# A thought stage with its normalisation behind the first product, and a grouped mixture whose rows are placed choice by choice

## The chip, the cores and the metric

The kernel runs on one core of one Trainium2 chip. The metric is device time in microseconds; the kernel before took 2209.59 us (median of 3 runs, 2209.09 to 2212.38).

## The reference, cut to what matters

Four layers, each with cross attention and a feed-forward part, act on x of 4 batches x 256 tokens x 256. Two of the eight parts are changed.

Layer 1's feed-forward, from the last token of each batch (the "thought"):

```
x_norm = layer_norm(x, in_gamma, in_beta)
thought = x_norm[:, -1, :] @ agg_w + agg_b              # 4 x 256
for _ in range(4):
    t = layer_norm(thought, pn_gamma, pn_beta)
    t = gelu(t @ d1_w + d1_b)                            # 4 x 1024
    thought = thought + (t @ d2_w + d2_b)
gate = sigmoid(x @ gate_w + gate_b)                      # 1024 x 256
out = x + gate * (thought @ bc_w + bc_b)[:, None, :]
x = x + layer_norm(out, out_gamma, out_beta)
```

Here x on the right is the normalised input. Layer 2's feed-forward is a mixture: 64 experts of width 176, of which each token chooses the 6 likeliest, and a shared part of width 352 that all tokens pass:

```
y = silu(x @ w1[e]) @ w2[e]          # for the 6 chosen e, mixed by their shares
shared = (silu(g) * u) @ shared_down # g, u = x @ shared_gate_up
```

All is float32.

## The kernel before, in words

The stages run one after another, each in a block of its own with one instruction list for each engine. A block's end holds all engines; nothing crosses it but DMAs issued ahead. Order within a stage is written out by hand: each engine's list is fixed, and semaphores (`wait_ge`) order the engines against each other. Tokens lie in 8 tiles (TT) of 128 rows; the width of 256 is 2 chunks (DC).

**Thought stage** (`thought_stage`, L1697). SP issues all loads in order, and last the four weights of the next attention (`Products.sync`, 5 MB). VectorE takes the moments of all 8 tiles (`Norm.vector`), then normalises the last tokens twice as 4 rows (`first_rows`, L1935), then the 8 tiles; TensorE transposes these (L199) and ScalarE copies them (L210). Each of the 4 steps is a chain: VectorE's statistics of the 4 thought rows, GpSimd's power for the inverse root (L1804), VectorE's rows (L1933), two transposes (`turn`, L1820), ScalarE's gamma and beta (L1901), the product with d1_w with its 4 spans in 4 column groups of TensorE (L1854), the bias on VectorE (L1965), Gelu (L1905), two transposes (L1860), a copy, the product with d2_w in 4 partial sums (L1865), a copy (L1909), and one product that adds the 4 parts (L1871). Behind that, TensorE does the step's two tiles of the gate product (L1833), and VectorE adds the gate's bias (L1949) and out_beta (L1951) in the next step. At the end come bc_w, a product that spreads each batch's row over 128 partitions (L1878), two copies (L1975), GpSimd's 8 products with the gate (L1808), VectorE's final normalisation in two halves (to L1998), and beside it, on TensorE and ScalarE, `Products` for the next attention's 16 heads (L406, L407, L411), in two banks by turns.

**Grouped stage** (`grouped_mixture`, L2198). Routing gives each (token, choice) a slot, with the experts in ascending order in blocks of 128 slots, 111 blocks at most. A token's 6 slots are sorted descending, so choice 0 is the highest. GpSimd writes the normalised rows to their slots with 48 indirect DMAs, tile by tile and in it choice by choice (L2490). Beside them VectorE makes 48 pairs of one-hots (L2580, L2581) that TensorE multiplies (L2396) to know each slot's target row. Then TensorE does the shared experts' outputs of pairs 0 and 1, the inputs of pairs 2 and 3 (L2336; 3 units a pair) and their outputs (L2346). SP loads each block's weights into 6 slots (L2304, L2307), each wait being on the block 6 before. ScalarE waits for all 48 placements (L2446), loads the rows of blocks 0 to 5 (L2444), and in the loop those of block b + 6. For each block TensorE transposes the rows (`turn`, L2354; two blocks ahead), multiplies (`up`, L2366; one ahead) and again (`down`, L2374, L2375); VectorE copies x_t (L2631), ScalarE applies silu (L2455) and copies y (L2464), GpSimd scatters y (L2496), behind its last placement.

Of the kernel before, what the change touches and what calls it, by code (L numbers as in the profile page):

```python
# [12 lines left out]
ACT = mybir.ActivationFunctionType  # L13
# [6 lines left out]
P = 128  # L20
# [93 lines left out]
class Norm:  # L114
# [29 lines left out]
    def vector(self, dve, between=None, after=None):  # L144
        m = self.m
        for n in range(self.SETS):
            of = self.set_of(n)
            for t in of:
                last = dve.bn_stats(self.stats[:, t, :], m.x[:, t, :])
            last.then_inc(self.stats_done, 1)  # L150
            dve.wait_ge(self.stats_done, n + 1)
            for t in of:
                last = dve.bn_aggr(self.moments[:, t, :], self.stats[:, t, :])
            last.then_inc(self.moments_done, 1)
            dve.wait_ge(self.moments_done, n + 1)
            at = slice(of[0], of[-1] + 1)
            dve.tensor_scalar(self.spread[:, at], self.moments[:, at, 1], self.EPS, None, ALU.add).then_inc(self.spread_done, 1)

        if between:
            between()  # L160
# [21 lines left out]
    def gpsimd(self, pool):  # L182
        for n in range(self.SETS):
            at = slice(self.set_of(n)[0], self.set_of(n)[-1] + 1)
            pool.wait_ge(self.spread_done, n + 1)
            pool.tensor_tensor(self.rstd[:, at], self.spread[:, at], self.m.minus_half[:, at], ALU.pow).then_inc(self.rstd_done, 1)
# [197 lines left out]
class Products:  # L384
# [4 lines left out]
    def __init__(self, st, m, dram, banks):  # L389
        self.m, self.banks = m, banks  # L390
# [7 lines left out]

    def tensor(self, pe, h):
# [3 lines left out]
        wait_for(pe, self.product_kept, h + 1 - len(self.banks))  # L403
        bank = self.banks[h % len(self.banks)]
# [4 lines left out]
    def scalar(self, act, h):  # L409
        act.wait_ge(self.product_made, h + 1)  # L410
        act.copy(self.m.products[:, h, :], self.banks[h % len(self.banks)][:]).then_inc(self.product_kept, 1)  # L411
# [1285 lines left out]
def thought_stage(nc, m, dram, of_heads):  # L1697


    eps = 1e-6  # L1700
# [5 lines left out]
    IN_GAMMA, IN_BETA, AGG_B, D2_B, BC_B = range(5)  # L1706
    small_names = ("in_gamma", "in_beta", "agg_b", "d2_b", "bc_b")
    GATE_B, OUT_GAMMA, OUT_BETA = range(3)
    wide_names = ("gate_b", "out_gamma", "out_beta")
    with Stage(nc, m, "l1f") as st:  # L1710
# [5 lines left out]
        to_group = st.sbuf("to_group", [chunks, span // P, groups, ROWS])  # L1716
# [1386 lines left out]
```

## Time and profile before

| What | us |
| --- | --- |
| Median of 3 runs | 2209.59 |
| The profiled execution | 2207.66 |
| Its span | 2205.9 |
| Thought stage, 822.9 to 906.8 | 83.9 |
| Hidden sums of its steps start | 846.4, 857.8, 868.5, 879.1 |
| Grouped stage's first placement, first block's transposes | 1290.1, 1357.3 |

A row of a timeline is the start in us, how long, engine, line, operation, output and inputs by the program's names, shapes and how many records; in brackets the idle time before it and what released it. A float32 product leaves two records. PEclk is TensorE's granted clock as a share of 2.4 GHz. A stretch's row gives busy time for each engine. The profile was taken on one execution.

### The profile page before, as it was taken

The page shows a single profiled execution, that of the slowest core. Times are in us where ns is not written, and L with a number is a line of the kernel's source. Part 1 is how long each engine was busy: PE and PEld are TensorE (multiplying, and loading weights), DVE is VectorE, ACT ScalarE, POOL GpSimd, SP SyncE. Part 2 cuts the span into 40 slices and gives each one's busy share as a digit, 9 for nine tenths or more (in the row PEclk, how much of TensorE's full clock was granted, in tenths as well). Part 3 has the DMA queues.
Part 4 walks back from the last instruction along what each step waited for, and adds up shares of the span by engine and source line. Part 5 has one row for each costly group of instructions (what it writes and reads, how often), then busy time and mean ns, then how long its engine had stood idle before and what let it go on. Part 6 is the DMA issues. An engine that isn't in the chain of part 4 may idle for free. (4 is left out here: it accounts for less than half of the span.)

```text
span 2205.9 us, 43116 instructions
## 1 busy us (share of the span) xinstructions
PE 1994.0 (90%) x13031; PEld 1709.7 (78%) x13031; DVE 1500.8 (68%) x4243; ACT 1153.0 (52%) x2626; POOL 678.8 (31%) x1298
## 2 busy tenths in 40 slices
PE   5798796989999986799999885999879999988998
PEld 3544485779999983699999774999769999976887
DVE  6788576858878883788888772322268888875565
ACT  3656443756766752566666411444246666653333
POOL 3422102013333310333334155544323333312221
PEclk9899898999999996899999897999989999988999
DMA  2157302012212104520000024999810000014441
GB/s 67 33 109 196 129 1 72 2 56 71 78 52 78 56 17 155 183 88 0 0 0 0 29 95 159 315 318 315 282 41 23 14 21 14 15 32 122 117 116 39
DMA packets 145257, 193.66 MB, mean 88 GB/s; under 512 B 45084, under 2 KB 113284, under 8 KB 142216
## 3 DMA queue, kind: packets, MB, share of 16 engines
q1 hardware_dynamic: 119912, 152.40, 23.1%
q10 hardware_dynamic: 17584, 18.82, 2.6%
q0 software_dynamic: 7632, 20.85, 2.5%
q8 instruction: 66, 1.08, 0.2%
q14 instruction: 63, 0.52, 0.1%
HBM read 169.86 MB, written 56.62 MB: 103 GB/s over the span
## 5 line engine op out<-in xcount | busy, mean ns | idle before, releaser
L2631 DVE COPY l2f_x_t<-bank 128x256 f32<-128x256 f32 x111 | 47.1, 424 | 178.5 <-PE bank L2354 178.5
L2496 POOL DMA_INDIRECT l2f_y_rows<-l2f_y,l2f_target x111 | 111.6, 1005 | 115.9 <-ACT l2f_y L2464 113.7
L705 ACT ACTIVATE l1a_prob<-l1a_masked,l1a_shift,l1a_q_scale 128x512 f32<-128x512 f32 x128 | 104.5, 816 | 76.2 <-DVE l1a_shift L763 74.1
L705 ACT ACTIVATE l2a_prob<-l2a_masked,l2a_shift 128x512 f32<-128x512 f32 x128 | 92.8, 725 | 78.5 <-DVE l2a_shift L767 75.8
L705 ACT ACTIVATE l3a_prob<-l3a_masked,l3a_shift 128x512 f32<-128x512 f32 x128 | 92.7, 725 | 78.4 <-DVE l3a_shift L767 75.7
L2366 PE MATMUL bank<-l2f_x_t,l2f_w 128*128 128x128 f32 x888 | 118.4, 277 | 0.2 <-DVE l2f_x_t L2631 0.2
L1315 ACT ACTIVATE l0a_prob_t<-bank 128x512 f32<-128x512 f32 x128 | 76.2, 599 | 64.5 <-PE bank L1253 63.7
L2366 PEld LDWEIGHTS bank<-l2f_x_t,l2f_w 128*128 128x128 f32 x888 | 109.0, 193 | 0.6 <-issue 0.5
L1332 DVE TENSOR_REDUCE l0a_coarse<-bank 128x32 f32<-128x512 f32 x128 | 87.5, 688 | 26.1 <-PE bank L1243 24.4
L757 DVE CUSTOM_DVE_ANT_0 l3a_masked<-bank,l3a_side 128x512 f32<-128x512 f32 x128 | 88.4, 691 | 14.1 <-issue 12.8
L757 DVE CUSTOM_DVE_ANT_0 l2a_masked<-bank,l2a_side 128x512 f32<-128x512 f32 x128 | 88.4, 691 | 11.7 <-issue 10.4
L757 DVE CUSTOM_DVE_ANT_0 l1a_masked<-bank,l1a_side 128x512 f32<-128x512 f32 x128 | 88.4, 690 | 9.9 <-issue 8.6
L2699 POOL TENSOR_TENSOR l3f_low<-l3f_raw,l3f_high 128x768 fp32r<-128x768 f32 x24 | 44.3, 1848 | 160.5 <-ACT l3f_high L2694 160.5
L2455 ACT ACTIVATE l2f_h<-bank 128x128 f32<-128x128 f32 x111 | 30.8, 277 | 114.5 <-PE bank L2366 114.5
L2918 DVE TENSOR_TENSOR l3f_upped<-l3f_gate,bank 128x512 f32<-128x512 f32 x48 | 33.0, 687 | 78.0 <-PE bank L2819 78.0
L840 POOL TENSOR_TENSOR l3a_pool_woken<-ones 128x1 f32<-128x1 f32 x90 | 17.4, 193 | 210.8 <-ACT l3a_q_t L689 154.1
L779 DVE TENSOR_TENSOR l1a_prob_low<-bank,l1a_prob_high 128x512 fp32r<-128x512 f32 x128 | 81.1, 675 | 0.1
L779 DVE TENSOR_TENSOR l2a_prob_low<-bank,l2a_prob_high 128x512 fp32r<-128x512 f32 x128 | 81.1, 675 | 0.0
L779 DVE TENSOR_TENSOR l3a_prob_low<-bank,l3a_prob_high 128x512 fp32r<-128x512 f32 x128 | 81.1, 675 | 0.0
L2817 PE MATMUL bank<-l3g_x_high,l3f_high 128*128 128x512 f32 x192 | 75.8, 395 | 3.7 <-PEq L2033 3.7
L840 POOL TENSOR_TENSOR l1a_pool_woken<-ones 128x1 f32<-128x1 f32 x90 | 17.3, 192 | 195.9 <-ACT l1a_q_t L689 147.9
L840 POOL TENSOR_TENSOR l2a_pool_woken<-ones 128x1 f32<-128x1 f32 x90 | 18.3, 203 | 189.9 <-ACT l2a_q_t L689 165.1
(605 smaller groups left out, 7455.1 us busy)
## 6 DMA issues: line engine op xcount, KB each, us to landing
l2f_w<-w_rows SPq DMA_DIRECT2D x111, 304.0 KB
l1a_side<-rms SPq DMA_DIRECT2D x16, 1024.0 KB, 4.8
l2f_x_rows_of<-x_slots ACTq DMA_DIRECT2D x111, 128.0 KB, 3.9
w_rows<-in_l2f_w SPq DMA_DIRECT2D x4, 2048.0 KB
l2f_hots<-l2f_y_rows SPq DMA_DIRECT2D x8, 768.0 KB, 9.9
l3f_raw<-in_l3f_w SPq DMA_DIRECT2D x24, 256.0 KB, 3.8
l3f_mix<-shares SPq DMA_DIRECT2D x16, 384.0 KB, 3.8
l2f_w_rest<-in_l2f_w SPq DMA_DIRECT2D x111, 48.0 KB
```

What stands on the lines that cost most here:

```text
L705: act.activation(prob[:, unit, :], masked[:, unit, :], ACT.Exp, bias=shift[:, unit:unit + 1], scale=q_scale[:, slot, t:t + 1] if qk_norm e ...
L757: dve.tensor_tensor_reduce(masked[:, unit, :], score_bank[q][:], side[:, slot if qk_norm else 0, b * KEYS:(b + 1) * KEYS], 1.0, LOWEST, AL ...
L779: dve.tensor_tensor(prob_low[part], turn_bank[q][:].rearrange("p (n t) -> p n t", n=KT), prob_high[part].bitcast(F32), ALU.subtract).then_ ...
L840: pool.tensor_tensor(pool_woken[:], m.ones[:, 0:1], m.ones[:, 0:1], ALU.mult)
L1315: act.activation(prob_t[:, (2 * g + j) % slots, 2 * half:2 * half + 2, :], turned_bank[u % 2][:].rearrange("p (n t) -> p n t", n=2), ACT.E ...
L1332: dve.tensor_reduce(coarse[:, g % 2, j, q, :], score_bank[n % 3][:].rearrange("p (s k) -> p s k", k=LAST_KEYS), AX_X, ALU.max).then_inc(co ...
L2366: last = pe.matmul(pair_bank[b % 2][:, n * P:(n + 1) * P], w[:, slot, first:first + P], x_t[:, b % 2, c * P:(c + 1) * P], start=(c == 0), ...
L2496: pool.indirect_dma_start(y_rows, bass.IndirectOffsetOnAxis(target[:, b:b + 1], 0), y[:, b % of.Y_SLOTS, :], None).then_inc(y_stored[b % o ...
L2631: dve.tensor_copy(x_t[:, b % 2, :], turn_bank[b % 2][:, 0:D]).then_inc(x_kept, 1)
L2699: pool.tensor_tensor(self.low[:, slot, at], self.raw[:, slot, at], self.high[:, slot, at].bitcast(F32), ALU.subtract).then_inc(self.low_do ...
L2817: pe.matmul(bank[:], left_high, right_high, start=(c == 0), stop=False)
L2918: dve.tensor_tensor(upped[:, n, :], gate[:, n, :], up_bank[n][:], ALU.mult).then_inc(up_done, 1)
```

## The change

Two stages change, and each with several parts.

Thought stage:

- The thought is kept in two forms in two banks: as columns (`columns`, 128 x 2 x 32) and as rows (`thought`, each batch's row in all 32-row groups). Both are sums that TensorE accumulates: bias or residual come in as products with the identity (`ahead_t`, `ahead`), the partial sums with `sum_of` and `sum_all`.
- The normalisation moves behind the product with d1_w: the columns times gamma go in at once, and mean and inverse root are applied to the product, (hidden - mean x sums) x rstd + offsets, in two VectorE instructions. Sums (gamma @ d1_w) and offsets (beta @ d1_w + d1_b) are made once, in step 0.
- The first rows are normalised once instead of twice (the two layer norms folded), ahead of the second set of moments.
- The step's gate tiles go ahead of the transposes of `active`, and heads 0 and 1 of `Products` into steps 2 and 3.
- The end: four products with bc_w on spread columns (`batch_t`), one bank for each batch; VectorE multiplies gate tiles 0 and 1, GpSimd the other 6.
- Loads wait on seven semaphores instead of three; small ones are issued from ScalarE's queue.

Grouped stage:

- Placements go choice by choice, 5 to 0, with a semaphore each. SP loads rows of blocks 0 to 4 (`AHEAD`), block b as soon as choice 5 - b has landed, then weights of blocks 6 to 10, then, when choice 0 has landed, rows of blocks 5 to 10. TensorE does blocks 0 to 4 one after another; the old loop starts at block 5.
- The shared outputs of pairs 0 and 1 come into the one-hot loop at its products 1 and 3, the shared inputs of pairs 2 and 3 at 8, 13, ... 33; VectorE's share of that work comes 6 products later.

```diff
 def thought_stage, tensor:
-                    turn(1 + n)
-                    for c in range(DC):
-                        ... hidden_bank <- rows_t x d1_w
+                    pe.wait_ge(rows_set, n + 2)
+                    past_rows(hidden_bank, lambda c: rows_t[:, c, :]).then_inc(hidden_ready, 1)
+                    if n == 0:
+                        pe.wait_ge(set_up, 5)
+                        past_rows(parts_bank, lambda c: pn_rows[:, PN_GAMMA, c, :]).then_inc(sums_ready, 1)
+                        pe.wait_ge(bias_kept, 1)
+                        past_rows(active_bank, lambda c: pn_rows[:, PN_BETA, c, :], ends=False)
+                        for i in range(inner):
+                            last = pe.matmul(active_bank[:, i * P:(i + 1) * P], to_group[...], d1_rows[:], start=False, ...)
+                        last.then_inc(offsets_ready, 1)
+                        norm.ready(pe)
+                        pe.wait_ge(gate_loaded, 32)
+                    gate_products(step_tiles(n))
+                    for h in range(sum(BEHIND[:n]), sum(BEHIND[:n + 1])):     # BEHIND = (0, 0, 1, 1)
+                        products.tensor(pe, h)
                     pe.wait_ge(active_done, n + 1)
                     ... transposes of active
+                    pe.wait_ge(columns_kept, n + 1)
+                    pe.matmul(columns, m.ident[:], ahead_t[...], start=True, stop=False)
+                    if n + 1 < STEPS1:
+                        pe.wait_ge(rows_kept, n + 1)
+                        pe.matmul(thought, m.ident[:], ahead[:], start=True, stop=False)
                     pe.wait_ge(active_kept, n + 1)
                     ... product with d2_w
                     pe.wait_ge(parts_kept, n + 1)
-                    pe.matmul(row_bank[0:B, 0:D], sum_of[:], parts[:], start=True, stop=True).then_inc(product_ready, 1)
-                    gate_products(step_tiles(n))
+                    for to in range(DC):
+                        last = pe.matmul(columns[:, to * ROWS:(to + 1) * ROWS], parts[:, to * P:(to + 1) * P], sum_of[:], ...)
+                    last.then_inc(thought_ready, 1)
+                    if n + 1 < STEPS1:
+                        pe.matmul(thought, sum_all[...], parts[:], start=False, stop=True).then_inc(rows_ready, 1)
 ...
+                for b in range(B):
+                    if b >= 2:
+                        pe.matmul(said_of(b), ones_row[:], bc_b[:], start=True, stop=False)
+                    pe.wait_ge(batch_set, b + 1)
+                    for c in range(DC):
+                        last = pe.matmul(said_of(b), batch_t[:, b, c, :], weights["bc_w"][:, c, :], start=False, ...)
+                    last.then_inc(said_ready, 1)
+                for h in range(sum(BEHIND), HEADS):
+                    products.tensor(pe, h)
 vector:
+                def turn_thought(n):
+                    dve.wait_ge(thought_ready, n + 1)
+                    dve.tensor_tensor(rows_t[:], columns..., pn_rows[:, PN_GAMMA, :, :], ALU.mult).then_inc(rows_set, 1)
+                def measure_thought(n):
+                    dve.wait_ge(rows_ready, n + 1)
+                    dve.bn_stats(stats[:], thought).then_inc(stats_read, 1)
+                    dve.wait_ge(stats_read, n + 1)
+                    link(dve.bn_aggr(moments[:], stats[:]))
+                    dve.tensor_scalar(spread[:], moments[:, 1:2], eps, None, ALU.add).then_inc(spread_done, 1)
+                norm.take_moments(dve, 0)
+                ... first rows from last_x: one normalisation, gamma, beta
+                norm.take_moments(dve, 1)
+                dve.wait_ge(set_up, 5)
+                turn_thought(0)
+                measure_thought(0)
+                norm.normalise(dve)
                 for n in range(STEPS1):
+                    if n:
+                        turn_thought(n)
+                        measure_thought(n)
                     dve.wait_ge(hidden_ready, n + 1)
+                    link(dve.scalar_tensor_tensor(centred[:], minus_sums[:], moments[:, 0:1], hidden_bank[...], ALU.mult, ALU.add))
+                    dve.wait_ge(rstd_done, n + 1)
+                    dve.scalar_tensor_tensor(hidden[:], centred[:], rstd[:], offsets[:], ALU.mult, ALU.add).then_inc(hidden_set, 1)
+                    dve.tensor_tensor(ahead_t[...], columns..., d2_columns..., ALU.add).then_inc(columns_kept, 1)
+                    if n + 1 < STEPS1:
+                        dve.tensor_tensor(ahead[:], thought, wide[:, D2_B, :], ALU.add).then_inc(rows_kept, 1)
+                    gate_sums(step_tiles(n))
+                    ... in the last step VectorE copies parts; in steps 1 and 2 it adds out_beta to 4 tiles each
 def grouped_mixture, sync:
-                for b in range(blocks):
+                for b in range(of.W_SLOTS):
+                    load_weights(b)
+                for b in range(of.AHEAD):                    # AHEAD = 5
+                    sp.wait_ge(x_placed[chosen - 1 - b], 16 * TT)
+                    load_rows(sp, b)
+                for b in range(of.W_SLOTS, of.W_SLOTS + of.AHEAD):
+                    load_weights(b)
+                sp.wait_ge(x_placed[0], 16 * TT)
+                for b in range(of.AHEAD, of.AHEAD + of.X_SLOTS):
+                    load_rows(sp, b)
+                for b in range(of.W_SLOTS + of.AHEAD, blocks):
                     load_weights(b)
 tensor, behind one-hot product n:
+                        if n in shared_in_at:                # 8, 13, 18, 23, 28, 33: units 6 to 11
+                            shared_in(shared_in_at[n])
+                        if n in shared_out_at:               # {1: 0, 3: 1}
+                            shared_out(shared_out_at[n])
 ...
-                turn(0)
-                turn(1)
-                up(0)
-                for b in range(blocks):
+                for b in range(of.AHEAD):
+                    turn(b)
+                    up(b)
+                    down(b)
+                turn(of.AHEAD)
+                turn(of.AHEAD + 1)
+                up(of.AHEAD)
+                for b in range(of.AHEAD, blocks):
 scalar:
-                act.wait_ge(x_placed, 16 * TT * chosen)
-                for b in range(of.X_SLOTS):
-                    load_rows(b)
 gpsimd:
-                for t in range(TT):
-                    for k in range(chosen):
+                for k in reversed(range(chosen)):
+                    for t in range(TT):
                         pool.indirect_dma_start(x_slots, ..., m.x_n[:, t, :], None).then_inc(x_placed[k], 16)
 vector, behind one-hots n:
+                    if n - of.SHARED_LAG in shared_out_at:   # SHARED_LAG = 6
+                        add_shared(shared_out_at[n - of.SHARED_LAG])
+                    if n - of.SHARED_LAG in shared_in_at:
+                        shared_multiply(shared_in_at[n - of.SHARED_LAG])
```

## Rows read from the trace of the kernel before

**Rows 1.** Page, part 1: busy us (share of span) xinstructions.
```profile
PE 1994.0 (90%) x13031; PEld 1709.7 (78%) x13031; DVE 1500.8 (68%) x4243; ACT 1153.0 (52%) x2626; POOL 678.8 (31%) x1298
```

**Rows 2.** Busy time by stretch: length, each engine busy (x records), clock, DMA.
```profile
822.90:906.80 83.90, 58.45 (x321) 34.64 (x321) 42.19 (x128) 25.46 (x58) 14.27 (x20) 0.72 0.32 103
...
841.00:852.00 11.00, 6.00 (x39) 2.01 (x39) 1.93 (x7) 3.28 (x7) 0.53 (x1) 0.50 1.07 354
```

**Rows 3.** Timeline, thought stage's opening and step 0: start, us, engine, line.
```profile
826.98 0.17 DVE L157 TENSOR_SCALAR l1f_norm_spread<-l1f_norm_moments 128x4 f32<-128x4 f32 x1
...
834.98 4.28 PE L199 MATMUL bank<-ident,l1t_x_n 128*128 128x128 f32 x14
...
844.34 1.93 PE L1854 MATMUL bank<-l1f_d_w,l1f_rows_t 128*32 128x256 f32 x16 [0.75 <-ACT l1f_rows_t L1901]
...
851.84 3.78 PE L1833 MATMUL bank<-l1f_gate_w,l1t_x_t 128*128 128x256 f32 x8
```

**Rows 4.** Line L1965: count, ns min/median/max, first and last start.
```profile
L1965 DVE TENSOR_TENSOR l1f_hidden<-bank,l1f_d_b x4: 423/424/425, 846.4 to 879.1; 128x256 f32<-128x256 f32 x4
```

**Rows 5.** Timeline, thought stage, last step.
```profile
873.96 3.14 PE L1833 MATMUL bank<-l1f_gate_w,l1t_x_t 128*128 128x256 f32 x8
...
875.39 0.53 POOL L1804 TENSOR_TENSOR l1f_rstd<-l1f_spread,minus_half 4x1 f32<-4x1 f32 x1 [10.48 <-DVE l1f_spread L1931]
...
878.01 1.07 PE L1854 MATMUL bank<-l1f_d_w,l1f_rows_t 128*32 128x256 f32 x16 [0.69 <-ACT l1f_rows_t L1901]
...
879.15 0.42 DVE L1965 TENSOR_TENSOR l1f_hidden<-bank,l1f_d_b 128x256 f32<-128x256 f32 x1 [0.99 <-PE bank L1854]
...
880.98 1.07 PE L1865 MATMUL bank<-l1f_d_w,l1f_active_t 128*32 128x256 f32 x16 [0.46 <-ACT l1f_active_t L1907]
...
883.06 1.99 PE L1833 MATMUL bank<-l1f_gate_w,l1t_x_t 128*128 128x256 f32 x8
```

**Rows 6.** Timeline, thought stage's end.
```profile
889.09 1.29 DVE L1975 COPY l1f_said<-bank 128x512 f32<-128x512 f32 x2 [2.08 <-PE bank L1878]
...
890.46 6.25 POOL L1808 TENSOR_TENSOR l1f_gate<-l1f_gate,l1f_said 128x256 f32<-128x256 f32 x8 [14.53 <-DVE l1f_said L1975]
...
894.46 0.59 ACT L411 COPY products<-bank 128x512 f32<-128x512 f32 x1 [0.29 <-PE bank L407]
...
903.28 3.25 DVE L1998 SCALAR_TENSOR_TENSOR x<-l1f_out,l1f_out_rstd,x 128x256 f32<-128x256 f32 x8
...
905.38 0.59 ACT L411 COPY products<-bank 128x512 f32<-128x512 f32 x1 [0.29 <-PE bank L407]
```

**Rows 7.** Busy time by stretch, grouped stage.
```profile
1332.00:1357.00 25.00, 0.03 (x1) 0.00 (x0) 0.42 (x1) 0.00 (x0) 16.47 (x18) 0.60 0.30 102
1400.00:1575.00 175.00, 175.00 (x1241) 161.53 (x1241) 43.89 (x113) 71.01 (x266) 84.45 (x89) 1.00 0.97 314
```

**Rows 8.** Line L2490, the row placements, and their time to landing.
```profile
L2490 POOL DMA_INDIRECT x_slots<-l2g_x_n,l2f_slot_i x48: 956/960/1465, 1290.1 to 1352.7; - x48
...
DMA to landing us min/median/max: 2.4/2.4/4.6
```

**Rows 9.** Timeline, grouped stage.
```profile
1312.18 0.96 POOL L2490 DMA_INDIRECT x_slots<-l2g_x_n,l2f_slot_i  x1 [0.30 <-issue]
...
1316.33 10.52 PE L2336 MATMUL bank<-l2g_x_t,l2f_shared_w 128*128 128x256 f32 x48
...
1326.69 5.34 PE L2346 MATMUL bank<-l2f_shared_w,l2f_shared_h 128*128 128x256 f32 x24
...
1355.11 2.76 ACTq L2444 DMA_DIRECT2D l2f_x_rows_of<-x_slots  x6
...
1357.33 1.09 PE L2354 MATMUL bank<-ident,l2f_x_rows_of 128*128 128x128 f32 x4 [25.29 <-DMA l2f_x_rows_of<-x_slots]
...
1362.89 0.37 ACT L2464 COPY l2f_y<-bank 128x256 f32<-128x256 f32 x1 [0.44 <-PE bank L2375]
```

**Rows 10.** Line L2396, the one-hot products.
```profile
L2396 PE MATMUL bank<-l2f_hots x96: 275/362/555, 1289.8 to 1311.0; 128*128 128x111 f32 x96
```

More of the change, by code:

```diff
@@ L1705, in thought_stage @@
     span = HIDDEN1 // groups
[L1706 to L1709, printed above, removed]
+    inner = span // P
+    GATE_B, OUT_GAMMA, OUT_BETA, D2_B = range(4)
+    PN_GAMMA, PN_BETA = range(2)
+    BEHIND = (0, 0, 1, 1)
     with Stage(nc, m, "l1f") as st:
@@ L1763, in step_tiles @@
+        columns = columns_bank[:, 0:DC * ROWS]
+        thought = thought_bank[:, 0:D]
         def step_tiles(n):
@@ new lines, in _ @@
+                pe.matmul(columns, bias_columns[:], to_chunk[:].rearrange("c g r -> c (g r)"), start=True, stop=False)
+                pe.matmul(thought, ones_row[:], bias_rows[:], start=True, stop=False)
+                pe.wait_ge(turn_kept, 1)
+                for to in range(DC):
+                    for c in range(DC):
+                        last = pe.matmul(columns[:, to * ROWS:(to + 1) * ROWS], weights["agg_w"][:, c, to * P:(to + 1) * P],
+                                         first_t[:, c, :], start=False, stop=(to == DC - 1 and c == DC - 1))
@@ L1840, in _ @@
+                last.then_inc(thought_ready, 1)
+                for c in range(DC):
+                    for g in range(groups):
+                        last = pe.matmul(thought[g * ROWS:(g + 1) * ROWS, :], first_t[:, c, :], weights["agg_w"][:, c, :],
+                                         start=False, stop=(c == DC - 1), tile_position=(0, g * ROWS))
+                last.then_inc(rows_ready, 1)
+                pe.wait_ge(d1_loaded, 96)
                 pe.transpose(active_bank[0:chunks, 0:P], d1_columns[:], m.ident[:]).then_inc(bias_turned, 1)
@@ L1898, in _ @@
+                act.wait_ge(offsets_ready, 1)
+                act.copy(offsets[:], active_bank[:, 0:span]).then_inc(offsets_kept, 1)
                 for n in range(STEPS1):
[L1899 to L1903 removed]
@@ L1913, in _ @@
                     act.activation(gate[:, t, :], raw[:, t, :], ACT.Sigmoid).then_inc(gate_done, 1)
-                for h in range(HEADS):
+                for b in range(1, B):
+                    act.wait_ge(said_ready, b + 1)
+                    act.copy(said[:, b, :], said_of(b)).then_inc(said_kept, 1)
+                for h in range(sum(BEHIND), HEADS):
                     products.scalar(act, h)
@@ L2144 @@
     EARLY = 2
+    AHEAD = CHOSEN - 1
+    SHARED_LAG = 6
     BY_PRODUCT = 3
@@ L2379, in _ @@
                 pe.wait_ge(shared_loaded, 16)
-                shared_in(0)
+                for n in range(of.SHARED):
+                    shared_in(n)
                 pe.wait_ge(masked, 1)
```

428 lines of the change are left out of this document (225 added, 203 removed).

## The prediction

> **What bounds the kernel now.** I read the page first: TensorE is busy for 90% of the span [rows 1], but that is a mean over the whole program, so the question is how busy it is where the change works. Second, busy time by stretches: in the thought stage (822.9 to 906.8) TensorE shows 58 of 84 us at a mean granted clock of 0.72, and in its first step the clock is 0.50, the 1.2 GHz level [rows 2]. Third, the timelines, for what ends each wait. Everything before and behind either stage waits at a block boundary, so a microsecond cut inside one comes off the total.
>
> Thought stage. The four steps form one chain: hidden sums start at 846.4 and for the last time at 879.1, a pitch of 10.9 us [rows 4], with one small instruction at a time. The stage ends at 906.53, VectorE's last update of x (903.28 + 3.25), just behind ScalarE's last product copy at 905.97 [rows 6].
>
> Grouped stage. The 48 row placements on GpSimd start at 1290.1 and the last at 1352.7 [rows 8]; TensorE ends its shared-expert work at 1332.03 (1326.69 + 5.34) and starts the first expert block at 1357.33, after 25.3 us of waiting for rows [rows 9]; from 1332 to 1357 it has 0.03 us of work [rows 7]. The 111 blocks then run on TensorE at 100%: 1241 records in 175 us, 14 records a block, so 1.974 us a block [rows 7].
>
> **The change, thought stage.**
>
> Opening. The first rows now take one normalisation with the two folded together, and VectorE's second set of moments (ending 827.15 before [rows 3]) comes behind them: I put it at 831.0. GpSimd's inverse root and to_group copy follow it (1.5), so the fifth set_up comes at 832.5, VectorE's rows at 832.8, its statistics until 834.3. The token transposes then start at 834.8, against 834.98 before [rows 3]: they are the bound, because ScalarE copies one tile in 0.6 us. They end near 839.5. On ScalarE's queue nine small DMAs that SP issued before (0.45 each) and the Gelu table now stand ahead of its first copy, which I place at 829.3; nothing waits, with some 0.3 to spare, and what they'd hold beyond that, up to the d1_w landing, is in the lower bound. The first hidden sums now need three products with d1_w in place of one: 1.93 us each at the low clock [rows 3], the third nearer 1.5 as I expect the clock to rise, plus the bias product and a copy: 839.5 + 5.9 + 0.5 = 845.9. Gain 0.5; bounds from -2 (pn columns landing late hold both ScalarE and the transposes) to +2.
>
> One step. Before, from the row sum being ready (873.96, where the gates start) to the hidden sums at 879.15 took 5.2 us: statistics, GpSimd's 0.53 root, rows, two transposes with 4 columns, two affine copies, and the product of 1.07 [rows 5]. After, from the column sum: one multiply (0.25), then the product (1.07) beside statistics and root, then the centring of 0.42: 2.05 us. The second half, 879.15 to 883.06, was 3.9 us [rows 5]. After, TensorE has two gate tiles queued between the first product and the transposes: 1.99 us at the full clock [rows 5] against 1.4 us of centring, hidden and Gelu, so the transposes wait 0.45; the identity products that carry the residual add 0.15 beside ScalarE's copy, the column product takes 0.3. So 4.35, and a step is 2.05 + 4.35 = 6.4 us. In steps 2 and 3 a head's product lies there too, 0.9 us, the pitch of ScalarE's copies (894.46 to 905.38 is 12 heads, 0.91 each [rows 6]): 7.3. Hidden 0 to hidden 3: 6.4 + 6.4 + 7.3 = 20.1, against 32.7: gain 12.6. The gate sums and out_beta additions (0.34 to 0.42 each) lie on VectorE beside this; they cost nothing while a step is over 5.5 us.
>
> End. Last hidden to last sum: 3.9 becomes 5.3 (gates and a head in front of the transposes), loss 1.4. Last sum to end: before 883.06 to 906.53, 23.5 us. After, four batches are spread by VectorE and multiplied by TensorE (0.9 each, 0.45 for the late biases), the last ready 5.05 us after the sum; said copies lie on ScalarE. VectorE's end: first gates at 1.85, GpSimd's remaining six products of 0.78 (6.25 for 8 [rows 6]) until 7.7, then adds, statistics, gain and 3.25 of updates: 16.7. The other end: 14 heads behind 5.05 at 0.91, plus a copy: 18.4. So the products are late next and set the end: gain 5.1.
>
> Sum at the full clock: 0.5 + 12.6 - 1.4 + 5.1 = 16.8 us. The clock is the weak term. It rose in the old stage behind each pair of gate tiles (which took 3.78 us at the low clock, 1.99 at full [rows 3, 5]) and fell again within the step. A step is now 90% TensorE (5.8 of 6.4), but its products with 32-column tiles look like those during which it fell. All of it at 1.2 GHz costs 38 us more (below); I take 9% of that, 3.3 us. Gain 13.5; bounds 8 and 19.
>
> **The change, grouped stage.** Shared experts. Before, 21.2 us of shared work stand behind the one-hots: outputs of pairs 0 and 1 (5.3), inputs of pairs 2 and 3 (10.52), their outputs (5.34, to 1332.03) [rows 9]. Only the last 5.3 stay behind. One-hots come every 0.44 us (48 from 1289.8 to 1311.0 [rows 10]) and cost TensorE about 0.28 at full clock (two records at 175/1241), so the loop holds 7.7 us of the 15.9 moved in; the first output runs at the low clock (2.5 more) and VectorE waits for it. The loop ends at about 1321.5, the shared work at 1327; bounds 1326 and 1334.
>
> Blocks ahead. Choice by choice, each choice is 8 issues. The pitch is 1.26 us (1312.18 to 1352.7, 32 issues), so the 40th starts at 1342.6; it lands 2.4 later [rows 8, 9], SP loads block 4's rows and TensorE has them 2.2 us after the issue, as 1355.11 to 1357.33 [rows 9]: 1347.3. A block alone takes at most 5.5 us (1357.33 to 1362.89 [rows 9]) at the low clock. Blocks 0 to 3 fit between 1327 and 1347, block 4 ends by 1352.8, before the last choice lands (1355.1): all five are free. Gain 5 x 1.974 = 9.9.
>
> What it gives back. SP issues the weights of blocks 6 to 10 only behind block 4's rows, from about 1345.5: 5 x 352 KB at 314 GB/s [rows 7] is 5.6 us of transfer beside the last 8 placements and in front of block 5's rows in SP's queue. Behind that wait stand rows 5 to 10 and all later weights. Placements landed in 2.4 us alone and up to 4.6 beside weight loads [rows 8]: between 0 and 2.2 us late; I take 1.0, nearer the median. A warmer clock at block 5 may return up to 1.5. Gain 8.9; bounds 5.5 and 11.5.
>
> A rule that speaks against this: by the Trainium skill, SBUF — State Buffer, "SBUF: two separate sides", a VectorE instruction in a two-port mode locks GpSimd out and so holds up descriptors of its DMAs. The trace agrees: the 16 issues beside the one-hots took up to 1.465 us against 0.956 alone, a pitch of 1.47 against 1.26 (3.1 us lost) [rows 8, 9]. If each placement paid for the longer loop too, the last would start 0.8 us later; as the one-hots stay 96 instructions, I leave the sum as it is.
>
> **Sum.** 13.5 + 8.9 = 22.4 us. The profiled execution took 2207.66 us (span 2205.9): 2185.3. The median is 1.9 above it, so 2187.
>
> **Rivals.**
> 1. The clock stays low in half of the thought stage. For: 0.50 in step 0, 0.72 overall [rows 2]. Against: the gaps that went with it (row normalisation, GpSimd's root) leave TensorE's path. It costs 38/2 less the 3.3 already taken: 15.7 us, total 2203, 0.3% faster.
> 2. Slower: TensorE at 1.2 GHz all through the stage, with gates queued in front of each transpose. Place: product 1.93, gates 3.78 [rows 3], transposes 0.7, identities 1.15, product 1.93, sums 0.6, copies 0.85: 11.5 a step, 13.3 with a head; last sum at 893.3, said 9.2, 14 heads at 1.75, end 927.5: 21 us later than 906.5, less 8.9: 2222. It decides once over two thirds of TensorE's work from 839 on runs low (it may lose 38; both gains at full clock are 25.7). Against: a denser queue than any old step. By the Trainium skill, TensorE: Matmul & The Clock Gate, "What's actually happening", the low clock is the default and recent activity lifts it; that rule gives the full clock here, 2184, and the trace's rise behind dense gate tiles agrees.
> 3. The head start is given back: the last choice and block 5's rows land late by the 2.2 and VectorE's stalls in the loop push the shared work to 1334, so that block 4 ends behind them. Grouped gain 3 to 4, total 2192.
> 4. The change doesn't do what it says: placements by choice don't free early blocks. The waits show they do (block b waits for choice 5 - b alone), so this would be 2196, with little weight.
>
> **How the numbers follow.** Forecast 70% (own range 2178 to 2192); rival 3 and 4 12%; rival 1 10%; rival 2 and milder forms of it 8%. A difference under 0.2% (4.4 us) can't be told from none. Slower: 5%; within 0.2%: 5% (between rivals 1 and 2); faster: 90%. The range 2177 to 2199 leaves out rivals 1 and 2.
>
> **What would show it.** Hidden sums' starts (centring) at pitches of 6.4, 6.4 and 7.3, first at 846; 10 would refute the step. Granted clock near 0.9 from 850 on. The stage's last instruction a product copy, not VectorE's update, near 893. First block at 1327 (shifted by the thought gain), a gap before block 4, and block 5 at most 2 us later against the last placement than block 0 was; steady block still 1.97. Wrong if the pitch stays above 9, if ScalarE or pn's landing holds the opening, or if steady blocks slow down.

## The result, and the profile after

The changed kernel took 2230.27 us (median of 4 runs, 2227.91 to 2234.98) against 2209.34 before: a ratio of 1.0067, 95% interval 1.0037 to 1.0097. (The medians alone make 1.0095; the ratio on record is the smaller one, and both lie in the interval.) Its four runs of before are the three of the first table and one of 2206.14; the record names no chip for these runs. Forecast was 2187. It is slower, by about 1%, outside the range and on the other side. Later runs of the same file on chip 13 took 2181.66 us; both results hold, and why there are two is the subject of what follows.

The profiled execution took 2228.92 us, span 2226.9. Page, part 1 (busy us, share, instructions); it is within 1% of [rows 1] on every engine, so the loss is in waits:

```profile
PE 1996.5 (90%) x13117; PEld 1716.8 (77%) x13117; DVE 1499.1 (67%) x4244; ACT 1152.2 (52%) x2622; POOL 674.9 (30%) x1297
```

**Thought stage: as forecast, or better.** The hidden sums' line, the stretch up to the stage's end with 841 to 852 for [rows 2], two of the products with d1_w, which begin a step, and the stage's last instructions on VectorE and ScalarE:

```profile
L2051 DVE SCALAR_TENSOR_TENSOR l1f_hidden<-l1f_centred,l1f_rstd,l1f_offsets x4: 483/484/486, 845.2 to 865.3; 128x256 f32<-128x256 f32 x4
```

```profile
822.90:893.00 70.10, 57.32 (x407) 38.82 (x407) 42.96 (x140) 24.70 (x55) 13.22 (x20) 0.88 0.43 128
841.00:852.00 11.00, 10.51 (x105) 6.59 (x98) 4.06 (x13) 1.92 (x5) 0.56 (x1) 0.95 1.08 324
```

```profile
856.35 1.07 PE L1857 MATMUL bank<-l1f_d_w,l1f_rows_t 128*32 128x256 f32 x16
...
863.67 1.07 PE L1857 MATMUL bank<-l1f_d_w,l1f_rows_t 128*32 128x256 f32 x16
```

```profile
885.65 2.85 DVE L2094 SCALAR_TENSOR_TENSOR x<-l1f_out,l1f_out_rstd,x 128x256 f32<-128x256 f32 x7
...
889.52 0.59 ACT L421 COPY products<-bank 128x512 f32<-128x512 f32 x1 [0.30 <-PE bank L417]
```

The first hidden sum is at 845.2 (846.4 before [rows 4]) and the last at 865.3 where 879.1 stood. The two products are 7.3 us apart; the four hidden sums start at 845.15, 851.60, 858.02 and 865.35, pitches of 6.4, 6.4 and 7.3. The granted clock is 0.88 over the stage (0.72 before [rows 2]) and 0.95 where it was 0.50. ScalarE's product copy (889.52 + 0.59 = 890.11) ends the stage, 16.4 us before 906.53 [rows 6], and the first placement comes 17.3 us earlier:

```profile
L2606 POOL DMA_INDIRECT x_slots<-l2g_x_n,l2f_slot_i x48: 957/961/1369, 1272.8 to 1333.0; - x48
```

**Grouped stage: 38.3 us lost** (17.3 gained before it, 21.0 lost in the span). Columns of the timelines are those of [rows 3]. TensorE, where L2453 is the shared units' input product and L2515 the one-hot product. In the brackets "issue" is idle time for which the profile shows nothing that the engine waited for, and "remote" a wait that ended with a semaphore update for which it shows no instruction:

```profile
1283.13 1.91 PE L2453 MATMUL bank<-l2g_x_t,l2f_shared_w 128*128 128x256 f32 x8
...
1285.98 1.73 PE L2453 MATMUL bank<-l2g_x_t,l2f_shared_w 128*128 128x256 f32 x7
1288.06 0.38 PE L2453 MATMUL bank<-l2g_x_t,l2f_shared_w 128*128 128x256 f32 x1 [0.35 <-issue]
1289.48 0.35 PE L2515 MATMUL bank<-l2f_hots 128*128 128x111 f32 x1 [1.04 <-issue]
1291.60 0.26 PE L2515 MATMUL bank<-l2f_hots 128*128 128x111 f32 x1 [1.78 <-issue]
1305.14 2.29 PE L2515 MATMUL bank<-l2f_hots 128*128 128x111 f32 x8 [13.28 <-issue]
1307.22 2.75 PE L2453 MATMUL bank<-l2g_x_t,l2f_shared_w 128*128 128x256 f32 x6
1310.57 0.38 PE L2453 MATMUL bank<-l2g_x_t,l2f_shared_w 128*128 128x256 f32 x1 [0.60 <-issue]
1313.37 0.58 PE L2453 MATMUL bank<-l2g_x_t,l2f_shared_w 128*128 128x256 f32 x1 [2.42 <-issue]
1316.18 0.34 PE L2515 MATMUL bank<-l2f_hots 128*128 128x111 f32 x1 [2.22 <-issue]
1318.97 0.34 PE L2515 MATMUL bank<-l2f_hots 128*128 128x111 f32 x1 [2.46 <-issue]
1342.29 2.09 PE L2515 MATMUL bank<-l2f_hots 128*128 128x111 f32 x8 [22.98 <-DVE l2f_hots L2710]
```

ScalarE, the only user of those units' products:

```profile
1303.54 0.38 ACT L2556 ACTIVATE l2f_shared_gate<-bank 128x256 f32<-128x256 f32 x1 [35.12 <-remote]
1303.82 0.37 ACT L2557 COPY l2f_shared_up<-bank 128x256 f32<-128x256 f32 x1
1340.69 0.38 ACT L2556 ACTIVATE l2f_shared_gate<-bank 128x256 f32<-128x256 f32 x1 [36.51 <-remote]
```

SP, issuing weights:

```profile
1281.65 0.69 SPq L2412 DMA_DIRECT2D l2f_w<-w_rows  x1
1283.07 0.32 SPq L2415 DMA_DIRECT2D l2f_w_rest<-in_l2f_w  x1
1285.91 0.00 SPq L2412 DMA_DIRECT2D l2f_w<-w_rows  x1
1287.33 0.69 SPq L2415 DMA_DIRECT2D l2f_w_rest<-in_l2f_w  x1
```

Unit 6's product ends at 1285.04 (1283.13 + 1.91), but ScalarE takes it up at 1303.54, 18.5 us later; unit 7's ends at 1288.44 and is taken up at 1340.69. VectorE and then TensorE wait behind ScalarE. And TensorE is slow without waiting for anyone: from 1288 its instructions come one by one, 1.4 to 2.1 us apart, and from 1310 2.80 us, with the idle time marked "issue", and that inside one unit that has no wait in it. SP does the same: 1.42 or 2.84 us between issues that were 0.3 to 1.4 us apart, and no wait on a semaphore stands between these weights either. The matmuls themselves last no longer. GpSimd goes on at its 1.26 us. So it isn't one wait but nearly everything that the other engines do, until some 6.7 us after GpSimd's last placement (1333.0 + 0.96). The placements' own transfers are not slowed: 20 to 60 us behind the first, a packet of their queue takes 126 ns in the mean, and 125 in e13, a run without the stall (row 4 below). The same two stretches as in [rows 7], one in the placements and one of steady blocks:

```profile
1290.00:1330.00 40.00, 6.73 (x19) 4.93 (x19) 2.76 (x11) 0.65 (x2) 30.54 (x32) 0.58 0.35 118
1400.00:1550.00 150.00, 150.00 (x1064) 138.47 (x1063) 44.01 (x110) 61.10 (x228) 75.23 (x77) 1.00 0.98 317
```

TensorE works 6.7 of those 40 us. (The steady blocks keep 1.974 us: 150 us with 1064 records, 14 a block, make 1.974.) What comes behind: the last shared outputs, block 0's transposes, and block 5's:

```profile
1358.38 5.36 PE L2463 MATMUL bank<-l2f_shared_w,l2f_shared_h 128*128 128x256 f32 x24
1364.30 0.41 PE L2471 MATMUL bank<-ident,l2f_x_rows_of 128*128 128x128 f32 x2 [0.56 <-issue]
```

```profile
1386.75 1.12 PE L2471 MATMUL bank<-ident,l2f_x_rows_of 128*128 128x128 f32 x4 [4.35 <-DMA l2f_x_rows_of<-x_slots]
```

Block 5 starts at 1386.75; before it was due at 1357.33 + 5 x 1.974 = 1367.2 [rows 7, 9]. These 19.6 us are the result but for 1.4.

### The profile page after: what moved, and what is told of

Same layout as the page of the kernel before. It is cut to its first block and busy times, and to the rows that moved or that the text cites. A ratio compares the mean times of both kernels' runs of the same rounds, so it can differ in the third digit from the quotient of the medians.

```text
span 2226.9 us, 43289 instructions
## 1 busy us (share of the span) xinstructions
PE 1996.5 (90%) x13117; PEld 1716.8 (77%) x13117; DVE 1499.1 (67%) x4244; ACT 1152.2 (52%) x2622; POOL 674.9 (30%) x1297
## 5 line engine op out<-in xcount | busy, mean ns | idle before, releaser
L850 POOL TENSOR_TENSOR l2a_pool_woken<-ones 128x1 f32<-128x1 f32 x90 | 18.4, 205 | 189.3 <-ACT l2a_q_t L699 164.6
```

The costliest lines, as they stand in the source:

```text
L850: pool.tensor_tensor(pool_woken[:], m.ones[:, 0:1], m.ones[:, 0:1], ALU.mult)
```

## The experiments

18 runs of 12 different kernels were made, in five rows, each row on one chip beside runs of the kernel before; the results name the chip. "Stall" is short for the slowing just shown. Each table gives median us, and the ratio to before on the same chip with its 95% interval.

**Row 1, chip 15: the parts.** Theories B (placement order or SP's row loads stall the others), C (the shared units in the one-hot loop do) and D (the thought part only moves the code). Edits: e1 takes the thought stage of after with the grouped stage of before, e2 the reverse, and

```
# e3: after, shared work behind the loop
-    shared_out_at = {1: 0, 3: 1}; shared_in_at = {8 + 5 * n: ...}
+    shared_out_at, shared_in_at = {}, {}    # shared_out(0), shared_out(1), shared_in(6..11) behind it
# e4: after, placements and rows as before, AHEAD = 0
-                for k in reversed(range(chosen)):
-                    for t in range(TT):
+                for t in range(TT):
+                    for k in range(chosen):
```

> The thought stage of the changed kernel in front of the grouped mixture of the kernel before. The first placement came 17.3 us earlier in the changed kernel, so if the thought part is sound and its gain survives, 2207.7 - 17.3 = 2190 us (2188 to 2195). If instead the thought part only shifts the instruction streams and that is what stalls ScalarE in the grouped stage (theory D, position of the code), the stall of some 35 us shows here too and the time is above 2205 us.

> The grouped mixture of the changed kernel behind the thought stage of the kernel before. Theories B and C (the stall belongs to the grouped change itself): the 38.3 us that the grouped stage lost come back, 2207.7 + 38.3 = 2246 us (2240 to 2250), with ScalarE idle some 35 us twice ahead of the shared units 6 and 7. Theory D (position of the code): no stall, 2207.7 - 9 = 2199 us.

> The changed kernel with the shared experts' units taken out of the one-hot loop again, to their old place behind it; choice-by-choice placements and five serial blocks stay. Theory C (the shared units inside the loop make VectorE and TensorE wait on a ScalarE that does not answer while rows are placed): the loop runs through at its old pace of some 0.45 us per one-hot; the shared work behind it may still meet the silence of ScalarE, but at most until 6.7 us after the last placement (1334 + 7 = 1341), so at most some 30 us of it stay; without any stall 2190 us or below. Theory B (the order of the placements or SP's row loads between them): ScalarE, TensorE and SP stall as in the changed kernel, 2225 to 2235 us.

> The changed kernel with placements tile by tile, rows loaded by ScalarE's queue once all have landed and no serial blocks, as before; only the shared units stay in the one-hot loop. Theory C (units in the loop): stall as in the changed kernel, 2225 us or more. Theory B (order of placements, SP's row loads between them): no stall, 2190 us (2187 to 2194).

| Kernel | us | ratio (before: 2207.15) |
| --- | --- | --- |
| e1_thought | 2190.28 | 0.9927 (0.9910 to 0.9943) |
| e2_grouped | 2196.16 | 0.9953 (0.9936 to 0.9969) |
| e3_shared_behind | 2185.91 | 0.9908 (0.9891 to 0.9924) |
| e4_rows_as_before | 2190.75 | 0.9920 (0.9904 to 0.9937) |

None of the four stalls. The thought part is worth 16.9 us and the grouped part 11.0 by themselves, and e1's first placement is where after has it:

```profile
1272.83 1.26 POOL L2586 DMA_INDIRECT x_slots<-l2g_x_n,l2f_slot_i  x1 [3.63 <-DVE l2f_part L2671]
```

I missed with all three: B expected a stall in e2 and e3, C in e2 and e4, D in e1. It seemed to need the whole change; I took the kernel for the cause and did not think of the chip.

**Row 2, chip 7: small shifts of the whole.** D again, and E (the relative timing of the engines).

```
# e5: after, unchanged
# e6
+                    sp.wait_ge(x_placed[0], 16 * TT)        # ahead of each of the first five row loads
# e7: on each engine in the thought stage
+                for _ in range(128): engine.wait_ge(<reached>, ...)    # long reached
# e8: on GpSimd ahead of the placements
+                for n in range(5): pool.memset(idle[:, n, :], 0.0)
```

> The changed kernel once more, beside the three below and on their chip. If the stall is a fixed property of this program, 2230 us (2226 to 2235) again with ScalarE's shared units 6 and 7 some 35 us late each; if it was a rare event of one chip, 2180 us.

> The changed kernel, with SP's first five loads of rows (blocks 0 to 4) held until the last choice has been placed; placement order and shared units in the loop stay. Theory B (SP's loads of rows between the placements block the other engines' waits): no stall in the loop, but the five blocks lose their cover, 2190 us. If the loads are innocent (theories D and E): stall as before, 2225 us or more.

> The changed kernel with 64 more instructions on every engine's stream in the thought stage (waits on semaphores that have long been reached), so that all code of the grouped stage lies 4 KB further on, while the order of its instructions and its timing against each other stay. Theory D (place of the code: a refill of an instruction stream meets the placements): the stall goes or moves, 2180 to 2195 us with up to 10 us for the padding. Theory E (relative timing of the engines around the placements): stall stays, 2230 to 2240 us.

> The changed kernel with five small memsets on GpSimd ahead of its first placement (some 2 us), so that the placements start later against the one-hot loop; the code of the other engines lies where it did. Theory E (relative timing): the stall goes or changes its place, 2180 to 2190 us. Theory D (place of the code): stall as before, 2230 us.

| Kernel | us | ratio (before: 2216.6) |
| --- | --- | --- |
| e5_again | 2227.73 | 1.0037 (0.9995 to 1.0078) |
| e6_rows_late | 2228.63 | 1.0058 (1.0021 to 1.0094) |
| e7_padded | 2248.42 | 1.0144 (1.0114 to 1.0173) |
| e8_placed_later | 2235.56 | 1.0086 (1.0057 to 1.0115) |

All four stall, with two late pickups by ScalarE that sum to 71.7 to 73.2 us of idle time (71.6 in after). (e7's padding itself moves the first placement by 16.0 us.) So holding SP's row loads (B), moving the code (D) or some 2 us on GpSimd (E) does not take the stall away. (e8 is 7.8 us slower than e5; its two runs leave open why.) That the kernel before was 9.4 us slower here than in row 1 was in the table too, and I passed over it.

**Row 3, chip 13: single suspects.** F (semaphore updates come too thick), G (six semaphores), H (which rows are written), C' (the chain through ScalarE).

```
# e9: .then_inc(x_placed[chosen - 1], 16) for all 48; SP waits for 16 * TT * chosen before block 0's rows
# e10
-                    for t in range(TT):
+                    for t in reversed(range(TT)):
# e11
+                sp.wait_ge(x_placed[chosen - 1], 16 * TT)    # ahead of the first six weights
# e12: shared_in_at = {}; units 6 to 11 behind the loop, the outputs of pairs 0 and 1 stay in it
```

> The changed kernel, with all 48 placements counted on one semaphore again and SP's first rows loaded when all have landed; the choice-by-choice order and the shared units in the loop stay. Theory G (the six semaphores, one for each choice): no stall, 2185 to 2195 us on a chip where before takes 2207. Theory F (the semaphore updates of placements in this order, of the weights' transfers and of the loop come too thick, and TensorE's increments wait in line; the number of semaphores is no matter): stall as in the changed kernel, 20 us and more above before.

> The changed kernel, placements choice by choice but with the tiles of each choice from the last to the first, so that other rows of the slot table are written at each moment. Theory H (the stall comes of where the rows land in memory at that moment): it goes or changes, 2180 to 2195 us. Theory F: stall as before, two waits of ScalarE of some 72 us in all.

> The changed kernel, with SP's first six weight transfers held until the first choice has been placed (some 12 us later). Theory F (too many semaphore updates at once, in the 12 us in which placements and weights land together with the loop's start): the loop gets some units through before the weights come, and the stall starts only with them or not at all, 2180 to 2210 us. If the weights have no part in it: stall as before at the same place.

> The changed kernel, with only the two down products and their four adds inside the one-hot loop; the shared units 6 to 11 (TensorE, ScalarE, VectorE in turn) behind it as before. Theory C' (the loop must not hold a chain through ScalarE): no stall, 2183 to 2190 us, as with all shared work behind the loop (2186). Theory F: TensorE and VectorE are stalled all the same, 2200 us or more.

| Kernel | us | ratio (before: 2206.82) |
| --- | --- | --- |
| e9_one_semaphore | 2210.20 | 1.0020 (1.0009 to 1.0032) |
| e10_tiles_reversed | 2180.90 | 0.9886 (0.9858 to 0.9915) |
| e11_weights_late | 2181.73 | 0.9890 (0.9862 to 0.9919) |
| e12_outs_only | 2181.51 | 0.9899 (0.9868 to 0.9930) |

None stalls, though F had expected a stall in e9, e10 and e12. e9's units run on time too; it takes 29 us more than e10 because block 0's rows wait for all placements while five blocks still run one at a time: block 5 starts at 1368.00, and at 1339.53 in e10. But four different edits that all "cure" a stall cure nothing. e6 and e9 run the same instructions in the first microseconds of the placements, and only e6's engines slow down there. What was left was the chip, or the session in which a row was run.

**Row 4, chip 13: the kernel or the chip.** M (the stall belongs to the program) against L (to the chip or the session). The four kernels are after, e10, e9 and e2 unchanged.

> The changed kernel itself, in one row with the three below on one chip, since the kernels that stalled and those that did not have so far been run on different chips. Theory L (the stall belongs to the chip or the session): on a chip where the three below don't stall this one doesn't either, 2181 us where before takes 2207. Theory M (the stall belongs to the program, down to small differences): it stalls again, 2228 us, beside the others that don't.

> The changed kernel with the tiles of each choice placed from the last to the first, once more. Theory M: no stall again, 26 us below before (2181 where before takes 2207). Theory L: it goes as the changed kernel beside it goes, whichever that is.

> The changed kernel with one semaphore for all placements and rows loaded after all, once more. Theory M: no stall of ScalarE in the loop again, some 3 us above before, the wait for rows alone. Theory L: as the changed kernel beside it; with the stall the time is 2228 us or more.

> The grouped change alone behind the old thought stage, once more. Theory M: no stall again, 11 us below before. Theory L: as the changed kernel beside it; with the stall some 40 us above that.

| Kernel | us | ratio (before: 2207.29) |
| --- | --- | --- |
| e13_after_again (after) | 2181.66 | 0.9881 (0.9864 to 0.9897) |
| e14_reversed_again (e10) | 2183.98 | 0.9897 (0.9881 to 0.9914) |
| e15_one_semaphore_again (e9) | 2210.01 | 1.0015 (1.0004 to 1.0025) |
| e16_grouped_again (e2) | 2194.93 | 0.9952 (0.9930 to 0.9975) |

M is out: the changed kernel, to the letter, takes 25.6 us less than before. In its trace (e13) the rows that answer to those of after above: placements, TensorE's last shared outputs with the transposes of blocks 0 and 5, ScalarE at unit 6, and the same 40 us:

```profile
L2606 POOL DMA_INDIRECT x_slots<-l2g_x_n,l2f_slot_i x48: 956/960/1367, 1271.8 to 1332.0; - x48
```

```profile
1305.68 2.97 PE L2463 MATMUL bank<-l2f_shared_w,l2f_shared_h 128*128 128x256 f32 x13
1309.20 0.41 PE L2471 MATMUL bank<-ident,l2f_x_rows_of 128*128 128x128 f32 x2 [0.56 <-issue]
...
1340.49 0.69 PE L2471 MATMUL bank<-ident,l2f_x_rows_of 128*128 128x128 f32 x2 [4.03 <-DMA l2f_x_rows_of<-x_slots]
```

```profile
1283.92 0.39 ACT L2556 ACTIVATE l2f_shared_gate<-bank 128x256 f32<-128x256 f32 x1 [16.59 <-PE bank L2453]
```

```profile
1290.00:1330.00 40.00, 34.49 (x157) 27.84 (x157) 16.99 (x62) 4.69 (x18) 30.29 (x32) 0.77 0.40 130
```

ScalarE picks unit 6 up 16.6 us after unit 5, where after took 35.1; TensorE works 34.5 of the 40 us, where it worked 6.7.

**Row 5, chip 12: a chip that stalls.** after, and e12, which has no chain through ScalarE in the loop.

> The changed kernel once more, wherever it is run. The stall belongs to the chip: on a chip that stalls 2228 us or more, 11 to 20 us above before; on one that does not 26 us below before. No time between is expected.

> The changed kernel with the shared units 6 to 11 behind the one-hot loop (only down products and adds inside). On a chip that does not stall, 26 us below before as the changed kernel. On a chip that stalls: if ScalarE's part in the loop is needed for the stall, still some 25 us below before; if any kernel that places rows there is stalled, some 10 us above before, as the changed kernel.

| Kernel | us | ratio (before: 2217.71) |
| --- | --- | --- |
| e17_after_third (after) | 2231.57 | 1.0068 (1.0043 to 1.0094) |
| e18_outs_only_again (e12) | 2226.30 | 1.0045 (1.0027 to 1.0063) |

Two times and none between, as expected. And e18 stalls where the same kernel didn't on chip 13: 44.8 us more. Without a chain through ScalarE the slowing is bare: one-hot products, otherwise two records in some 0.45 us, come 2.1 to 2.8 us apart. Its timeline on TensorE and VectorE (L2711 and L2712 make a pair of one-hots), and its longest waits from 1272 to 1348 (us in total, times, longest):

```profile
1303.49 0.34 PE L2515 MATMUL bank<-l2f_hots 128*128 128x111 f32 x1 [2.27 <-issue]
1305.59 0.34 PE L2515 MATMUL bank<-l2f_hots 128*128 128x111 f32 x1 [1.76 <-issue]
1308.40 0.34 PE L2515 MATMUL bank<-l2f_hots 128*128 128x111 f32 x1 [2.46 <-issue]
1311.19 0.35 PE L2515 MATMUL bank<-l2f_hots 128*128 128x111 f32 x1 [2.45 <-DVE l2f_hots L2712]
```

```profile
1310.48 0.29 DVE L2711 TENSOR_SCALAR l2f_hots<-l2f_row,l2f_part 128x128 f32<-128x128 f32 x1 [1.06 <-issue]
1311.89 0.34 DVE L2712 TENSOR_SCALAR l2f_hots<-l2f_row,l2f_part,l2f_column 128x111 f32<-128x111 f32 x1 [1.12 <-issue]
1313.28 0.29 DVE L2711 TENSOR_SCALAR l2f_hots<-l2f_row,l2f_part 128x128 f32<-128x128 f32 x1 [1.05 <-issue]
```

```profile
PE bank L2515 <- issue: 25.9, 16, 2.5
...
DVE l2f_hots L2712 <- issue: 18.4, 20, 1.8
```

VectorE too is idle for "issue", and in the kernel no wait stands between these one-hots. So no wait between the kernel's engines explains it, and theory C' is out.

One more thing separates the runs that stall from the others. The trace records semaphore updates by engines and DMAs. Counted from the first placement:

```
us after the first placement      0-4   4-20   20-60
before (the profile shown first)   45    383     551
e13, chip 13, no stall             36    438     681
after, stall                       43     74      70
e5, chip 7, stall                  45     62      66
e17, chip 12, stall                41     65      64
e18, chip 12, stall                38     73      66
```

The counts fall some 4 us behind the first placement. SP's issues come late only from 1281.65 to 1283.07 on, 9 to 10 us behind it, and in e18 the one-hot loop keeps its full pace until some 17 us behind it. What is missing there are records and not updates: SP waits for 128 updates of the eight placements of choice 5 and goes on, and they leave 128 records in e13 and 38 in after. So in this stretch a wait can be marked "issue" only because its update wasn't recorded; the readings above rest on instructions that have no wait before them. But some updates are late in fact. TensorE's update for unit 6 is recorded at 1303.51, 0.03 us before ScalarE moves, though the product had ended at 1285.04, and that for unit 7 at 1340.67, 52 us after its product.

## Why the prediction was wrong

**Thought stage: right.** Forecast 16.8 at the full clock, 13.5 taken; the first placement came 17.3 us earlier, and e1 alone measured 16.9. Opening 0.5 forecast, 1.2 found (846.4 to 845.2). Steps 20.1 forecast, 865.3 - 845.2 = 20.1 found, with the pitches of the sum (6.4, 6.4, and 7.3 with a head's product). The products set the end; from the last hidden sum to it 23.7 were forecast (5.3 + 18.4) and 24.8 found. The 3.3 us kept back for a low clock were not needed: rivals 1 and 2 are refuted by 0.95 from 841 to 852. (The terms listed in rival 2 for a step at the low clock add up to 10.9 and not to the 11.5 that it uses; nothing hangs on it.)

**Grouped stage: near where it does not stall, in part by luck.** On chip 13 the shared work ended 36.9 us after the first placement (1308.65 against 1271.77); "the shared work at 1327" was 36.9 after 1290.1. The five blocks ran beside the placements, at up to 5.7 us each (5.5 taken as the most), the fifth done at 1336.5. Block 5 started 68.7 us after the first placement, where block 0 had started 67.2 after it [rows 8, 9]: 1.5 given back, 1.0 forecast, so 9.9 - 1.5 = 8.4 of gain against 8.9 forecast; e2 and e16 measured 11.0 and 12.4 with the stage alone. The 1.5 is a larger loss than the sum had, less a gain that it didn't have. The last placement came 2.4 us sooner after the first, and block 5 started 8.5 us behind the last placement where block 0 had started 4.6 behind it: 3.9 later, over the "at most 2 us" that was to show the prediction right. Of these 3.9, 1.7 are the landing (4.1 us in place of 2.4, to 1336.06), 1.5 are SP's queue, and 0.7 the transfer:

```profile
1336.63 0.33 SPq L2412 DMA_DIRECT2D l2f_w<-w_rows  x1
1337.16 0.33 SPq L2415 DMA_DIRECT2D l2f_w_rest<-in_l2f_w  x1
1337.54 2.86 SPq L2396 DMA_DIRECT2D l2f_x_rows_of<-x_slots  x6
```

Block 5's rows (L2396) stand behind the weights of block 10, and those wait for the end of block 4. All in all 25.6 us less than before on that chip, where 22.4 were forecast.

The rule I weighed stands in the Trainium skill, SBUF — State Buffer, "SBUF: two separate sides": while VectorE runs in a two-port mode, GpSimd cannot write its descriptors. The traces agree in so far as issues beside dense one-hots are longer, 1.47 us against 0.96 [rows 8]. The 0.8 us more that a longer loop might have cost did not come: spread over a longer loop, the one-hots held up mainly the first two placements, 1.37 us at most against 1.47 [rows 8], and the last came 60.2 us after the first, 2.4 sooner than before. It is the loop and not the order of the placements: both e1 and e4 place tile by tile, and take 63.0 us beside the short loop and 60.5 beside the long one.

**The step that failed** is "the loop ends at about 1321.5, the shared work at 1327; bounds 1326 and 1334". In the result the shared work ended at 1363.74, which is 90.9 us after the first placement in place of 36.9. Block 0 started 24.3 us later after the first placement than it had before. With it fell the next step, "all five are free": the five blocks cost 3.6 us each in the open instead of 1.974, and 4.35 us of waiting for block 5's rows came behind them, together 12.6 us more than before. That is 36.9 of the 38.3 us. The sum had one unstated premise: that engines which don't wait for a placement run beside the placements at their own pace. The profile of before shows just that, and nothing in it hints at the other; but it was one execution on one chip, and the 25.3 us in which TensorE waited for rows [rows 9], the one cover against such a slowing, were what the change set out to spend. The changed kernel takes 46 to 50 us more on chips 7 and 12 than on chip 13 (2227.73 and 2231.57 against 2181.66), the kernel before 9.4 to 10.4 more than on chips 15 and 13 (2216.6 and 2217.71 against 2207.15 and 2207.29). So the sign depends on where, or when, the kernel runs, and none of the rivals had this mechanism: what was moved under the placements comes back in full, because there almost nothing runs.

**Not settled.** Why the engines slow down on chips 7 and 12 and in the result, and not on 13 and 15. Chip and session are not told apart: chip 13 was used in two sessions and ran free in both, but no chip that stalls was used twice, and after itself never ran on chip 15. Nor does the kernel before fit well: beside the result it took 2206.14 to 2212.38, much as on the chips without a stall, and its profile shows none; as the record names no chip there, it can't be said whether it ran on the chip of the result. No trace of the kernel before from a chip that stalls is at hand, so whether its 10 us on chips 7 and 12 have the same cause is open. All timed runs here leave spans and clocks, so none shows whether the stall would be there with nothing recorded; that semaphore records are lost just before it makes the recording a suspect that wasn't cleared. Semaphore updates from the placements' DMAs may be what jams, since everything runs freely again at their end, but no experiment took them away. e1 to e4 were not run on a chip that stalls; whether the thought part alone, 17 us, is safe there is not shown. Of the two kernels that ran both with and without a stall, after and e12, neither beats the kernel before in both. On chip 13 the change as it stands is level with e10 to e12.

## What to carry to other kernels

Work moved under a long run of indirect DMAs is free only where the other engines run beside it, and here that differed between chips or sessions; before spending the last cover there, time the kernel on several chips. When a stall goes away with every edit, suspect where and when the kernels ran before what they hold, and run the unchanged one beside them each time: it was missing from rows 1 and 3 here. A median of before that moves by 9 us between two rows is a result too.

## What the runs showed of the hardware

- Two times for one program: 2181.66 us on chip 13, 2227.73 and 2231.57 on chips 7 and 12, each within 0.4% over its runs; whether it is the chip or the session is open.
- In the slowed stretch TensorE, VectorE and SP take steps of mostly 1.4 or 2.8 us (VectorE's one-hots in e18 1.40 apart, idle 1.1 for "issue"), while GpSimd keeps 1.26 us a placement; it ends 6.7 us behind GpSimd's last one.
- 48 placements are quicker beside sparser one-hots: 60.2 us beside a loop of 31.7 us (e13), 62.6 beside one of 21 (before).
- In the slowed runs the record of semaphore updates is thinned out: 38 of the 128 of one choice are there (after), though the wait on all 128 was passed.
